# Row-tiled spreading of the reciprocal denominators in a linear-attention kernel

## The reference

```python
xt = _gn(x) as tokens                     # B=16, N=6400, C=256
q, k, v = split(xt @ qkv_w.T + qkv_b)
q = relu(q); k = relu(k + pos_enc)
z = 1.0 / (einsum('bic,bc->bi', q, k.sum(axis=1)) + 1e-06)   # one z for each head and token
kv = einsum('bjc,bjd->bcd', k, v)
out = einsum('bic,bcd,bi->bid', q, kv, z)
y = x + (out @ proj_w.T + proj_b)
```

## Time and profile before

| | us |
|---|---|
| median of 3 runs | 2931.0 (2925.36 to 2931.67) |
| the profiled execution, its own time | 2934.1 |
| its span, first to last instruction | 2932.3 |
| mean granted TensorE clock | 0.989 |

### The profile page before, as it was taken

The page is one execution under the profiler, slowest core; times in us unless marked ns, Lnnn a source line. Parts: engine busy times, 40 slices in busy tenths (PEclk is TensorE's granted clock), DMA queues, the critical chain, the costliest instruction groups (busy, mean ns, idle before and its releaser), DMA issues.

```text
span 2932.3 us, 51480 instructions
## 1 busy us (share of the span) xinstructions
PE 2735.8 (93%) x16232; PEld 2309.1 (79%) x16232; DVE 2114.2 (72%) x2857; ACT 1756.6 (60%) x2565; POOL 1550.7 (53%) x998
## 2 busy tenths in 40 slices
PE   3889999999999999999999999999999999999997
PEld 2767878788787878878788787878878888787875
DVE  6657777676776767767777776777777776777775
ACT  2656666566665656656566665656656566665652
POOL 1435646455564555646455464555646455464554
PEclk9999999999999999999999999999999999999998
DMA  7556656475574655656466574655647466574655
GB/s 238 192 162 189 193 179 213 127 232 179 178 216 150 209 181 188 197 163 215 141 220 190 170 218 154 208 185 184 201 160 215 145 216 194 169 216 148 214 165 169
DMA packets 298195, 548.54 MB, mean 187 GB/s; under 512 B 21216, under 2 KB 41056, under 8 KB 297952
## 3 DMA queue, kind: packets, MB, share of 16 engines
q1 hardware_dynamic: 297952, 545.28, 58.9%
HBM read 433.79 MB, written 111.41 MB: 186 GB/s over the span
## 4 chain that ended last, share of the span: by engine, by line
PE 68%; DVE 11%; issue 10%; ACT 7%; POOL 3%; SPq 0%; DVEq 0%; ACTq 0%; DMA 0%; POOLq 0%
PE psX L482 15%; PE psK L420 15%; PE psX L442 14%; PE psG L432 10%; PE psG L434 5%; PE psT L411 5%; PE psX L458 3%; PE psX L468 2%; DVE kt L718 2%; ACT kt L939 2%; DVE kk L723 2%; ACT xn L916 1%; DVE swin L750 1%; POOL kacc L1074 1%; DVE zt L775 1%
## 5 line engine op out<-in xcount | busy, mean ns | idle before, releaser
L1060 POOL TENSOR_TENSOR hl<-xn,hl 128x512 fp32r<-128x512 f32 x386 | 503.2, 1325 | 705.1 <-ACT hl L928 705.1
L1074 POOL TENSOR_TENSOR kacc<-kacc,kt 128x512 f32<-128x512 f32 x368 | 535.8, 1456 | 539.7 <-ACT kt L939 539.7
L723 DVE TENSOR_TENSOR kk<-kt,kk 128x512 fp32r<-128x512 f32 x400 | 494.6, 1236 | 285.4 <-ACT kk L942 285.4
L420 PE MATMUL psK<-wqk,hl 128*128 128x256 f32 x4608 | 651.9, 292 | 10.1 <-DVE kt L718 8.8
L432 PE MATMUL psG<-kk,xt 128*128 128x512 f32 x1600 | 594.5, 405 | 32.1 <-DVE kk L723 31.8
L442 PE MATMUL psX<-hl,wqk 128*128 128x512 f32 x2304 | 599.3, 395 | 0.0
L420 PEld LDWEIGHTS psK<-wqk,hl 128*128 128x128 f32 x4608 | 581.2, 193 | 16.5 <-issue 14.3
L482 PE MATMUL psX<-uhl,mhl 128*128 128x512 f32 (+1 forms) x2400 | 565.3, 385 | 6.4 <-POOL uhl L1078 6.4
L939 ACT ACTIVATE kt<-kt 128x512 f32<-128x512 f32 x400 | 253.0, 632 | 523.8 <-DVE kt L718 516.1
L482 PEld LDWEIGHTS psX<-uhl,mhl 128*128 128x128 f32 x2400 | 440.2, 189 | 102.1 <-POOL uhl L1078 8.1
L442 PEld LDWEIGHTS psX<-hl,wqk 128*128 128x128 f32 x2304 | 407.8, 188 | 89.8
(11 more groups left out here) (88 smaller groups left out, 2635.8 us busy)
## 6 DMA issues: line engine op xcount, KB each, us to landing
xs<-in_x SPq DMA_DIRECT2D x198, 512.0 KB, 3.9
xa<-in_x SPq DMA_DIRECT2D x195, 512.0 KB, 4.6
xr<-in_x SPq DMA_DIRECT2D x192, 512.0 KB, 3.8
y<-xr SPq DMA_DIRECT2D x192, 512.0 KB, 4.8
posb<-pos_plus_bk SPq DMA_DIRECT2D x377, 256.0 KB, 2.8
posb<-in_pos SPq DMA_DIRECT2D x25, 256.0 KB, 2.7
pos_plus_bk<-posb SPq DMA_DIRECT2D x25, 256.0 KB, 3.1
q<-in_x SPq DMA_DIRECT2D x12, 512.0 KB, 5.7
```

The costliest lines, as they stand in the source:

```text
L420: last = mm(psK[:, i * C:(i + 1) * C], hl_of(t)[:, a, c, s:s + P], wqk[:, w, c, C:2 * C], start=(j == 0), stop=(j == len(terms) - 1))
L723: v.tensor_tensor(kk[:, hp, :, 1, :], kt[:, hp, :].rearrange("p (i n) -> p i n", i=TILES), kk[:, hp, :, 0, :], ALU.subtract).then_inc(kl_r ...
L1060: g.tensor_tensor(hl_of(t)[:, 1, :, s], xn[:, t % 2, :, s], hl_of(t)[:, 0, :, s], ALU.subtract).then_inc(xl_ready, 1)
L1074: g.tensor_tensor(both, both, kt[:, h % 2, :], ALU.add).then_inc(ks_done, 1)
```

## The change

Three places change. (1) The denominators of block t and half c go to quarter 2 (t mod 2) + c of the partitions, so each half has a quarter of its own; within a quarter the block's place is 4 s with s = (t mod 8) // 2. A round of four products is now two blocks with both halves, not four blocks with one half. (2) The spread product of a half takes only the 32 rows of its quarter, of `esel` and of `zmix`, where it took all 128; the two halves of a block use different quarters. `esel` shrinks from 16 matrices of 128 x 128 to 4. (3) In setup, a reduction over four groups of the loaded table and a copy take the place of the memset and of four additions; `kacc` is the scratch. Semaphores and waits of the loop are the same.

```diff
@@ -65,7 +65,7 @@
         wv = sb("wv", [P, CC, C])
         pw = sb("pw", [P, CC, C])
         bpb = sb("bpb", [P, CC, C])
-        esel = sb("esel", [P, 2, 4, CC, P], F32R)
+        esel = sb("esel", [P, 4, P], F32R)
         zt = sb("zt", [P, 2, BLK])
         zmix = sb("zmix", [P, 2, BLK], F32R)
         mhl = sb("mhl", [P, 2, CC, C], F32R)
@@ -106,7 +106,6 @@
         pos_stored = [sem(f"pos_stored{i}") for i in range(3)]
         pos_added = sem("pos_added")
         w_high = sem("w_high")
-        e_cleared = sem("e_cleared")
         m_reduced = sem("m_reduced")
         bvm_ready = sem("bvm_ready")
         bpb_done = sem("bpb_done")
@@ -447,16 +446,15 @@
                 pe.wait_ge(swin_ready, n + 1)
                 pe.wait_ge(q_saved, two_no(n, 7 if g == 0 else LAST, CC - 1))
                 blocks = range(8) if g == 0 else range(8, NBLK)
-                for s in range(2):
-                    for c in range(CC):
-                        w = WIN - 8 * s - 4 * c
-                        for j in range(4):
-                            t = 8 * g + 4 * s + j
-                            if t in blocks:
-                                k = size(t)
-                                final = t + 4 not in blocks and c == CC - 1
-                                last = mm(psX[32 * j:32 * j + 32, bank, 0:k], swin[:, c, w:w + 32], q_of(t)[:, c, :],
-                                          start=(s == 0 and c == 0), stop=final)
+                for s in range(4):
+                    w = WIN - 4 * s
+                    for quarter in range(4):
+                        t, c = 8 * g + 2 * s + quarter // 2, quarter % 2
+                        if t in blocks:
+                            k = size(t)
+                            rows = slice(32 * quarter, 32 * quarter + 32)
+                            last = mm(psX[rows, bank, 0:k], swin[:, c, w:w + 32], q_of(t)[:, c, :],
+                                      start=(s == 0), stop=(t + 2 not in blocks))
                 last.then_inc(den_done, 1)
 
             def spread_z(n, t):
@@ -465,7 +463,9 @@
                 if t in (0, 8):
                     pe.wait_ge(zm_ready, 2 * n + t // 8 + 1)
                 for c in range(CC):
-                    last = mm(psX[:, 2 + c, 0:k], esel[:, t % 8 // 4, t % 4, c, :], zmix[:, t // 8, 0:k],
+                    quarter = t % 2 * 2 + c
+                    rows = slice(32 * quarter, 32 * quarter + 32)
+                    last = mm(psX[:, 2 + c, 0:k], esel[rows, t % 8 // 2, :], zmix[rows, t // 8, 0:k],
                               start=True, stop=True)
                 last.then_inc(zb_done, 1)
 
@@ -854,7 +854,6 @@
             v.memset(zeps, Z_EPS)
             v.memset(kvm[:], 0.0)
             v.memset(swin[:], 0.0)
-            v.memset(esel[:].bitcast(F32), 0.0).then_inc(e_cleared, 1)
 
             def first_x(t):
                 dve.wait_ge(x_first[t % 4], 16 * (t // 4 + 1))
@@ -876,14 +875,12 @@
             v.tensor_reduce(out=nmask, in_=low_rows, axis=AX.XY, op=ALU.add).then_inc(m_reduced, 1)
             dve.wait_ge(m_reduced, 1)
             v.tensor_scalar(nmask, nmask, -1.0 / HD, None, ALU.mult)
-            dve.wait_ge(e_cleared, 1)
-            for top in range(2):
-                rows = slice(64 * top, 64 * top + 64)
-                for j in range(2):
-                    g = 8 * j
-                    hi = esel_raw[rows, g:g + 4, :].rearrange("p (s c) n -> p s c n", c=CC)
-                    lo = esel_raw[rows, g + 4:g + 8, :].rearrange("p (s c) n -> p s c n", c=CC)
-                    v.tensor_tensor(esel[rows, :, 2 * top + j, :, :], hi, lo, ALU.add)
+
+            places = kacc[:].rearrange("p i n -> p (i n)")
+            v.tensor_reduce(out=places, in_=esel_raw.rearrange("p (a s) n -> p (s n) a", a=4), axis=AX.X,
+                            op=ALU.add).then_inc(m_reduced, 1)
+            dve.wait_ge(m_reduced, 2)
+            v.tensor_copy(esel[:].rearrange("p s n -> p (s n)"), places)
             for t in range(4, NBLK):
                 first_x(t)
             dve.wait_ge(bpb_done, 1)
```

## The result

The changed kernel takes 2939.0 us (median of 14 runs, 2931.9 to 2947.6) where the kernel before takes 2931.8 (14 runs, 2921.8 to 2935.1). The ratio is 1.0027, 95% interval 1.0016 to 1.0038: slower by 7 us, 0.27% (0.16% to 0.38%). The forecast was 2941, 0.34% slower.

The account below looks back on a forecast made before the run. TensorE, busy 93% of the span, was taken as the bound. Spread steps +16.4 us over 15 batches, denominators -6.5 and setup 0 gave +9.9 us: 2941 us, 0.34% slower; 8-in-10 range 2887 to 2958.

Parts of the forecast that it names:

- The borders: Spread step (L468): switching to row tiles and back loses 0.10 us going in, 0.09 and 0.06 coming out; packed step +0.13.
- open load: Spread step: its first weights load with no product to hide under, 0.11 us; load and one stream together 0.34.
- One sign: Profile after: TensorE's idle time put down to issue ahead of L468 and L411 rises by some 0.1 us each.
- The overlap: Spread step: the two halves, in different row groups, stream at once, saving one stream of 0.23 us.
- without a border: Rival: row tiles at L468 start and end without loss, each counted step saves 0.23 us; 2890 us, chance 0.22.
- with half a border: Rival: the way in or out of the spread step is free; step -0.02 us, 2918 us, chance 0.13.
- without overlap: Rival: the spread step's halves run one behind the other, step +0.36 us; 2975 us, chance 0.08.
- without tiling: Rival: spread products not tiled at all, step stays 0.69 us, only the denominators gain; 2924.5 us, chance 0.02.
- Where it counts: Spread steps t = 4 to 12 count +0.13 us each, t = 2 -0.08, t = 0, 1, 3 hidden: +1.09 a batch.
- The denominators: L458, block 12: two products run as two pairs of passes instead of four in a row; -0.43 us a batch, -6.5 in all.
- Step t = 12: Last spread step before the loop's turn: counted in full at +0.13 us, the idle time behind it sliding with TensorE.
- Setup: VectorE before the loop: four additions (2.58 us) replaced by a 2.4 us reduction and a copy; net +0.3, taken as 0.

Follow-up runs that it names:

- e2: The changed kernel with both halves of a block taken from the first half's row group, so no overlap: 2962.4 us, ratio 1.0096 to the kernel before.
- e1: The changed kernel with the spread products whole again (128 rows), only the denominators' new places kept: 2921.2 us, ratio 0.9971 to the kernel before.
- e7: The kernel before with ten more 512-column products in step 12 of each batch: 2920.9 us in a single run.
- e10: The kernel before with ten more 512-column products in step 12 of each batch, timed again: 2922.4 us, ratio 0.9977 to the kernel before.
- e3: As e1, but each spread product takes 64 rows, both halves in the same 64: 2953.8 us, ratio 1.0080 to the kernel before.
- e5: The kernel before with four more 512-column products a batch: in step 8 2957.0 us, ratio 1.0064; in step 12 2946.9 us, ratio 1.0043.

## Why the prediction was right

- **The borders.** They were the step that decided, and they hold. Forecast for a packed step +0.13 us; measured 0.126, as the mean of eight. Each of its terms is there: in 0.09 (0.10), open load 0.11 (0.11), out 0.09 and 0.06 (0.09 and 0.06). The Trainium skill's "TensorEngine Tiling (Array Packing)", Key Properties, says that a change of the tiling mode drains TensorE. The runs agree so far as they show a loss at both borders for row tiles of 32 and of 64 rows. The Trainium skill's "TensorE: Matmul & The Clock Gate", LDWEIGHTS (loading the stationary operand), says that a load takes its time by the columns and not by the rows. The traces agree: 0.18 us for 32 and for 64 rows here, 0.19 for 128. One sign was put down wrongly: the idle time at the borders does not stand ahead of the products, whose modelled ends reach over it, but ahead of the loads, 62.4 us in 178 stretches at L468 where it was 1.5 us in two.
- **The overlap.** Full: e2 took it away and the step grew by 0.22. The rivals without a border, with half a border, without overlap and without tiling all fall on the four rows of the step. The reason given for half a border, that a product over fewer rows leaves the array sooner, has no support either: out of 64 rows the way back is as long as out of 32 (0.66 and 0.65 us from the first spread product to the transposes).
- **Where it counts.** Steps t = 4 to 11 in full, t = 0, 1 and 3 not: the table shows +0.17 at step 2 gone again by step 3 (with the denominators' gain, -0.50), and nothing left of t = 3 at step 4. The one at t = 2 starts out of its wait and gains as forecast: 0.43 us from its first product to the transposes and another 0.41 to the keys, where 0.57 and 0.35 stood before. The forecast for t = 0 to 11 with the denominators was 8 x 0.13 - 0.08 - 0.43 = +0.53; measured 0.52.

```profile
1474.36 0.50 PE L468 MATMUL psX<-zmix,esel 32*128 32x512 f32 x2 [1.15 <-ACT q L945]
1474.79 0.66 PE L410 MATMUL psT<-ident,xn 128*128 128x128 f32 x4
```

- **The denominators.** -0.43 forecast, 0.42 in the rows of the group, and -0.37 a batch in e1, whose batches have nothing else changed. The 0.05 between the two is not explained.
- **Step t = 12, wrong in sign.** I counted it with +0.13 since I took the idle time behind it to slide with TensorE. The work behind the second spread product already ran beside the branch, and the branch now starts 0.33 us behind the last L482 product where it was 0.47 (the 0.23 of the overlap, less 0.09): from step 12 to the branch 7.53 us, against 7.67. So, if the branch keeps its length, -0.14 in 13 turns, not +0.13 in 15 batches: 3.8 us too much.
- **Setup, mis-sized.** I took 0, from 2.4 us for a reduction of 2048 elements with a strided read at 0 to +2; it took 3.61, and the first transposes came 1.3 us late.
- **The sum by what was measured:** 15 x 0.52 - 13 x 0.14 + 1.3 = 7.3 us; the medians differ by 7.2. The misses are of opposite sign, and that the whole agrees so well is partly luck. The interval of the ratio allows 4.7 to 11.1 us, and the sum takes every batch to be like a full-clock one and the branches to be equally long. The single traces do not retrace it: from the first branch to the last it is 2296.2 us before and 2295.6 and 2296.4 in the two traces after, since the stretches between the branches are 4.0 and 4.3 us longer in all and the 13 branches 4.6 and 4.1 us shorter. From the first transposes to the first branch it is 3.3 and 5.1 us more, where 0.38 us a batch gives about 1; the same stretch scatters by as much between two traces of the kernel before with ten products more (500.0 us in e7, 495.5 in e10).
- **The range.** 2887 to 2958 was wide, since it had to reach over the rival without a border, and "slower" had a chance of 0.45. What the traces bear out is the mechanism of the step; the time by itself would not have told the forecast from its neighbours.

That the falls of the clock and the branches account for what is missing in e2, e3 and e5 is worked out from one trace each, not shown apart; e10 shows that they can be had or not with the same work in the rest of the batch.

## What to carry to other kernels

Row or column tiles can pay where many products of one tile shape stand together, as the denominators' four column tiles do, which start together round after round. Here each excursion into row tiles, with weights of 128 columns, costs 0.35 us on a packed TensorE, so one pair of 512-column products, which saves 0.23, is too few. Look for an operation that already starts out of a wait (-0.08 us at t = 2 here); to put all that is tiled side by side would share the borders, but was not run. When a change is smaller than what the loop's turn and the clock scatter, compare batches between turns and at full clock: 0.01 us of scatter there, some 10 us in the whole.

## What was not expected of the hardware

- The loop's branch on TensorE lasts 3.4 to 6.7 us in these traces, and what is queued before it runs beside it. The last one, which does not go back to the start of the loop, takes 0.08 us in the trace of before. The 13 idle stretches at the turns sum to 41.3 us before and 32.1 after, and the profile names no other engine for them:

```profile
PE psT L411 <- issue: 41.3, 13, 4.7
```

```profile
PE psT L410 <- issue: 32.1, 13, 4.9
```

- Ten needless products of 512 columns in each batch made the kernel 0.23% faster (0.13% to 0.33%), and with them the granted clock did not fall at any turn of the trace; four made it 0.43% slower (0.21% to 0.64%). The mean granted clock went from 0.989 to 0.996 with the ten, and was 0.988 with the four; over all timed runs it is 0.995 to 0.998 with the ten, against 0.988 to 0.992 of the kernel before beside them. What sets the branch's start and its length is open.
